# Distance attention of a two-layer decoder: scores by row halves, norms by bf16 pieces

## The chip, the cores and the metric

The kernel runs on one core of a Trainium2 chip. The metric is the time of the device in microseconds (us) for one whole execution. The engines are TensorE (PE, matrix products into the banks of PSUM), VectorE (DVE), ScalarE (ACT) and GpSimd (POOL), each with its own queue of instructions in fixed order; they wait for each other by semaphores. SyncE (SP) issues the DMAs.

## What is computed

A decoder of two layers over x of 4 batches x 512 tokens x 128 features. The change touches only the first attention, which has 16 heads of 64 features and weighs by distance:

```
P = LN(x) @ W_in + b_in                  # per head: Q, K, V, G of 64 features
d2 = q2[:, None] + k2[None, :] - 2 * Q @ K.T
W = (1e-4 + sqrt(max(d2, 0))) ** -2
A = (W / (1e-4 + W.sum(-1))) @ V
x = x + (G * A) @ W_out + b_out
```

q2 and k2 are the squared norms of the rows of Q and K. After it come a cross attention with ReLU, an attention with top-2 experts, and the second layer (window attention, cross attention, a quantized feed-forward); their instructions stay as they are. All matrix products of the first attention are fp32.

## The kernel before

**Units.** Stage A, the distance attention, is cut into 32 units u, one for each pair of heads p of each batch b (`divmod(u, PAIRS)`). A unit has 2 heads x 512 queries x 512 keys. Keys lie on partitions, queries along the free axis, so that a bank (128 keys x 512 queries) is one of eight score chunks c, numbered head by head (`hd, kt = divmod(c, QT)`).

**Scores.** One fp32 product over all 128 rows gives a whole chunk but for k2 (`scores`, L1910). Its 128 contraction rows are, for head 0, the 64 features of K above 64 rows of ones (`SK`), against the 64 features of -2Q above the 64 squares of Q (`MQ`); for head 1 the halves change places. So q2 comes out of the same product. For this the query projection is made twice with the weights written twice into WQ (keys QA and QB, L1891), once for each head with both row halves alike; VectorE scales one half (L2250) and ScalarE squares the other (`squares`, L2078). k2 comes from `key_norms` (L1899), a product of the squared keys with a constant of ones by head halves, and is copied to K2 (L2263).

**From scores to weights.** VectorE adds k2 and takes the maximum with 1e-30 (`guard`, L2272, one instruction a chunk, eight a unit) into D, which has two buffers. ScalarE takes for each head, four chunks together, the square root (L2084), the logarithm (L2092) and the exponential of -2 times it (L2100). Between root and logarithm, and between exponential and root, it loads another table. The logarithm and exponential of the row sums (`row_sums`, L2107 and L2111) and the squares of the next unit stand between the two large logarithms.

**Behind the weights.** GpSimd adds the four key chunks of each head by two instructions, 1024 and 512 columns (`sum_weights`, L2408, L2413). TensorE makes the weighted values (`weighted_values`, L1919, column halves: one head writes partitions 0 to 63, the other 64 to 127 of one bank) and, from GpSimd's sums, the row sums (L1925). ScalarE's inverse of them goes into the gates on GpSimd (`scale_gates`, L2420), VectorE multiplies gates and weighted values (`gated`, L2283), and TensorE adds the pair's piece of the output projection (`out_piece`, L1936).

**Order.** Each engine's order is written out by hand. On TensorE a turn of the loop over u is: scores(u); keys and values of u+1 (L1879, L1882); weighted values and row sums of u-1; queries (twice) and gates of u+1 (L1893), key norms of u+1; output piece of u-2; then the extra jobs of `after_batch`, which carry finished batches into the next layer norm and cross attention. PSUM banks are handed out in that order by `psum_jobs` and `place_jobs`: stage A rotates through banks 0 to 6 (pool A), bank 7 gathers the output pieces. `begin` makes TensorE wait until the reader of a bank's former user is done.

**The end of stage A.** Stage C (attention with experts) begins while the last unit is finished; `TAIL` says at which of its steps n a leftover of stage A is issued: weighted values and row sums of unit 31 (L1919, L1925) at n = 9, the gated values of unit 30 at n = 6. In stage C, L738 and L757 are bf16 products of 32 rows, L1016 reductions of them on VectorE, and L1144 to L1155 GpSimd's steps that split an fp32 operand into bf16 pieces.

## Time and profile before

| | |
|---|---|
| median of 3 timed runs | 1331.55 us (1330.48 to 1332.87) |
| the profiled execution | 1330.9 us, span of its trace 1329.1 us |
| TensorE busy in the span | 1209.8 us, 91% |
| VectorE | 959.5 us, 72% |
| ScalarE | 922.6 us, 69% |
| GpSimd | 509.4 us, 38% |
| chain that ended last | TensorE 78%, VectorE 12% |
| costliest groups | L2272, guards: 189.9 us; L1910, scores: 225.7 us; L2408, sums: 151.2 us |
| DMA | busy in the first two of 40 slices, then hardly |

Busy time is the time in which an engine has an instruction running; products on TensorE overlap, so a group's busy time is that of their union. The chain of waits goes back from the last instruction, at each step to what released it. An fp32 product is two instructions in the trace (x16 is eight products), each with its own load of weights (PEld). A form such as 128*64 128x512 is a product over 128 rows to 64 columns of the array, with 512 columns of the moving operand.

### The profile page before, as it was taken

The page shows a single profiled execution, that of the slowest core. Times are in us where ns is not written, and L with a number is a line of the kernel's source. Part 1 is how long each engine was busy: PE and PEld are TensorE (multiplying, and loading weights), DVE is VectorE, ACT ScalarE, POOL GpSimd, SP SyncE. Part 2 cuts the span into 40 slices and gives each one's busy share as a digit, 9 for nine tenths or more (in the row PEclk, how much of TensorE's full clock was granted, in tenths as well). Part 3 has the DMA queues.
Part 4 walks back from the last instruction along what each step waited for, and adds up shares of the span by engine and source line. Part 5 has one row for each costly group of instructions (what it writes and reads, how often), then busy time and mean ns, then how long its engine had stood idle before and what let it go on. Part 6 is the DMA issues. An engine that isn't in the chain of part 4 may idle for free.

```text
span 1329.1 us, 16572 instructions
## 1 busy us (share of the span) xinstructions
PE 1209.8 (91%) x5870; PEld 658.3 (50%) x5870; DVE 959.5 (72%) x1782; ACT 922.6 (69%) x1194; POOL 509.4 (38%) x359
## 2 busy tenths in 40 slices
PE   6999999999999999998888888899999999976765
PEld 3444544445454445542322222577775777743444
DVE  7876777777777778666888898236546787768895
ACT  3999999999999999993667777545554565633321
POOL 2554444545444545485445452023330000034233
PEclk9999999999999999996989999799998999979778
DMA  8200000000000000010000000000001000000000
GB/s 184 65 1 1 0 0 1 0 0 1 1 1 1 0 0 1 1 64 1 17 1 1 0 2 0 1 1 0 1 0 60 1 1 1 1 1 1 1 8 24
DMA packets 27709, 14.97 MB, mean 11 GB/s; under 512 B 16638, under 2 KB 26476, under 8 KB 27500
## 3 DMA queue, kind: packets, MB, share of 16 engines
q1 hardware_dynamic: 27628, 13.92, 3.9%
q8 instruction: 48, 0.79, 0.3%
q14 instruction: 33, 0.27, 0.1%
HBM read 12.86 MB, written 1.05 MB: 10 GB/s over the span
## 4 chain that ended last, share of the span: by engine, by line
PE 78%; DVE 12%; issue 5%; POOL 2%; ACT 2%; DMA 0%; POOLq 0%; SPq 0%; ACTq 0%; DVEq 0%
PE PS L1910 17%; PE PS L1919 9%; DVE ARENA L1016 5%; PE PS L882 4%; PE PS L1891 4%; PE PS L857 4%; PE PS L771 3%; PE PS L1237 3%; PE PS L722 3%; PE PS L1226 2%; PE PS L1221 2%; PE PS L1213 2%; PE PS L738 2%; PE PS L1936 2%; PE PS L1879 2%
## 5 line engine op out<-in xcount | busy, mean ns | idle before, releaser
L2272 DVE TENSOR_SCALAR ARENA<-PS,ARENA 128x512 f32<-128x512 f32 x256 | 189.9, 749 | 54.9 <-PE PS L1910 36.1
L1910 PE MATMUL PS<-ARENA 128*128 128x512 f32 x512 | 225.7, 594 | 2.4 <-issue 2.3
L2408 POOL TENSOR_TENSOR ARENA<-ARENA 128x1024 f32<-128x1024 f32 x64 | 151.2, 2363 | 126.0 <-ACT ARENA L2100 121.4
L1016 DVE TENSOR_REDUCE ARENA<-PS 128x1 f32<-128x512 f32 x256 | 161.0, 682 | 32.4 <-PE PS L738 32.0
L927 ACT ACTIVATE ARENA<-PS 128x1024 f32<-128x1024 f32 x128 | 128.4, 1026 | 50.2 <-PE PS L757 50.1
L1910 PEld LDWEIGHTS PS<-ARENA 128*128 128x128 f32 x512 | 95.0, 190 | 113.3 <-issue 111.1
L2084 ACT ACTIVATE ARENA<-ARENA 128x2048 f32<-128x2048 f32 x64 | 122.1, 1911 | 31.6 <-DVE ARENA L2272 31.2
L2092 ACT ACTIVATE ARENA<-ARENA,consts_sb 128x2048 f32<-128x2048 f32 x64 | 127.8, 1996 | 0.4
L1919 PE MATMUL PS<-ARENA 128*64 128x512 f32 x512 | 118.3, 604 | 0.9 <-DVE ARENA L2272 0.9
L2100 ACT ACTIVATE ARENA<-ARENA 128x2048 f32<-128x2048 f32 x64 | 118.4, 1898 | 0.0
L2250 DVE TENSOR_SCALAR ARENA<-PS,BT 64x512 f32<-64x512 f32 x64 | 48.0, 750 | 77.7 <-PE PS L1891 74.2
L2420 POOL TENSOR_TENSOR ARENA<-ARENA 128x512 f32<-128x512 f32 x32 | 40.7, 1273 | 162.8 <-ACT ARENA L2111 162.7
L1172 POOL TENSOR_TENSOR ARENA<-ARENA 128x512 f32<-128x512 f32 x32 | 40.6, 1269 | 142.1 <-DVE ARENA L1130 141.9
L738 PE MATMUL PS<-ARENA 32*128 32x512 bf16 x256 | 73.3, 409 | 20.6 <-DVE ARENA L1016 15.1
L2413 POOL TENSOR_TENSOR ARENA<-ARENA 128x512 f32<-128x512 f32 x64 | 82.1, 1283 | 5.0
L771 PE MATMUL PS<-ARENA 128*32 128x512 f32 x512 | 73.6, 648 | 10.6 <-issue 10.4
L963 ACT ACTIVATE ARENA<-PS,BN 128x512 f32<-128x512 f32 x64 | 43.0, 687 | 47.9 <-PE PS L857 47.8
L738 PEld LDWEIGHTS PS<-ARENA 32*128 32x128 bf16 x256 | 18.1, 92 | 102.2 <-DVE ARENA L1016 65.7
L882 PEld LDWEIGHTS PS<-W,ARENA 128*128 128x128 f32 x512 | 61.6, 192 | 12.9 <-issue 12.4
L1617 POOL TENSOR_TENSOR X<-X,W 128x512 f32<-128x512 f32 x4 | 6.0, 1498 | 159.7 <-DVE Y L2214 159.7
L1919 PEld LDWEIGHTS PS<-ARENA 128*64 128x64 f32 x512 | 34.5, 138 | 61.2 <-issue 57.6
L1891 PE MATMUL PS<-XT,WQ 128*128 128x512 f32 x128 | 63.4, 618 | 0.0
(268 smaller groups left out, 2469.7 us busy)
## 6 DMA issues: line engine op xcount, KB each, us to landing
ARENA<-in_window_bias_dram SPq DMA_DIRECT2D x1, 1536.0 KB, 6.6
WKVG<-in_L_attn_W_in_dram SPq DMA_DIRECT2D x3, 448.0 KB, 6.8
X<-in_x_dram SPq DMA_DIRECT2D x4, 256.0 KB, 4.8
W<-in_L_ffn_w_dram SPq DMA_DIRECT2D x1, 1024.0 KB
out_dram<-X SPq DMA_DIRECT2D x4, 256.0 KB, 2.2
WQ<-in_L_attn_W_in_dram SPq DMA_DIRECT2D x2, 448.0 KB, 8.0
BV<-in_L_attn_b_in_dram SPq DMA_DIRECT2D x1, 512.0 KB, 6.8
Wout<-in_L_attn_W_out_dram SPq DMA_DIRECT2D x1, 512.0 KB, 4.8
```

The source lines that it names most:

```text
L738: done(pe.matmul(begin(("cS", n, j)), STK[r, w % 4, 0, t * P:(t + 1) * P], STK[r, w % 4, 1, :], start=True, stop=True), ("cS", n, j))
L882: mm = pe.matmul(o[:, t * P:(t + 1) * P], H1[:, i % 2, c, t * P:(t + 1) * P], W2[:, e, c, :], start=c == 0, stop=c == 1)
L927: act.activation(PT[m % PT_SLOTS], bank(("cP", m)), ACT.Exp, scale=0.5).then_inc(sem("c_exp"), 1)
L1016: dve.tensor_reduce(NMX[:, w % 2, t, h:h + 1], bank(("cS", n, j)), AX.X, ALU.max, negate=True).then_inc(sem("c_max"), 1)
L1891: done(pe.matmul(o, w, XT[:, b], start=True, stop=True), (key, u))
L1910: done(pe.matmul(o, SK[:, hd, kt * P:(kt + 1) * P], MQ[:, hd, :], start=True, stop=True), ("S", u, c))
L1919: mm = pe.matmul(o[hd * 64:hd * 64 + 64, :], VA[:, u % 3, kt, hd * 64:hd * 64 + 64], D[:, u % 2, hd, kt, :], start=kt == 0, stop=kt == QT - 1)
L2084: act.activation(d, d, ACT.Sqrt).then_inc(sem("rooted"), 1)
L2092: act.activation(d, d, ACT.Ln, bias=const("eps_w")).then_inc(sem("logged"), 1)
L2100: act.activation(d, d, ACT.Exp, scale=-2.0).then_inc(sem("w_ready"), 1)
L2272: dve.tensor_scalar(D[:, u % 2, hd, kt, :], bank(("S", u, c)), K2[:, u % 2, kt, hd:hd + 1], 1e-30, ALU.add, ALU.max).then_inc(sem("guarded ...
L2408: pool.tensor_tensor(WPAIR, D[:, u % 2, hd, 0:2], D[:, u % 2, hd, 2:4], ALU.add).then_inc(sem("w_paired"), 1)
```

## The change

- Scores. A chunk is now the sum of two products in one bank: first three bf16 pieces of q2 (32 rows, of which `PIECES` has ones in three; each of four chunks has its own group of 32 rows), then the fp32 product over the 64 rows of a head, head 0 in rows 0 to 63 and head 1 in rows 64 to 127. Chunks are numbered by key block and then head, so heads alternate. Scores come in two groups of four, in each first the four pieces, then the four fp32 products. D has the key block ahead of the head, and ScalarE's two instructions of each kind cover two key blocks of both heads.
- Query norms. Queries are projected once (`project_pair`, with the keys), two units ahead; VectorE makes their square (times -2) from the bank, TensorE sums it by a product with `pairsum` (`query_norms`), VectorE scales it into QX, and GpSimd splits QX into the pieces by four instructions (`split_norms`), three units ahead in its queue. ScalarE's squares are gone; KSQ and QSQ come from `scalar_tensor_tensor` on a bank and SBUF.
- Order. Keys and queries of u+2, values and gates of u+1, weighted values and row sums of u-1, the extra jobs, the norms of u+2, the output piece of u-2. Gated values are those of u-2, ahead of the pair's evacuation. On ScalarE the row sums stand behind both large logarithms, with the extra jobs (`between`) between them and the exponentials. On GpSimd three sums of 1024 columns take the place of two of 1024 and two of 512, and the gates come last in a turn.
- Banks. Pool A has six banks, the weighted values bank 6 alone.
- Start and tail: unit 0 makes the pairs and norms of units 0, 1 and 2; gated30 stands at n = 5 and sums31 at n = 6. One of two DMAs for WQ goes, in each of the two parts of the weights. Scratch tiles share places (MSK with R1, MB with BXV).

The diff, cut; what it takes away is the code printed above.

```diff
+    piece = part % 32
+    cols["piece_drops_high"] = (piece >= 1).astype(np.float32)[:, None]
+    cols["piece_drops_mid"] = (piece == 2).astype(np.float32)[:, None]
+    cols["is_piece"] = (piece < 3).astype(np.float32)[:, None]
...
-TAIL = {"scores2": 1, "values0": 2, "gated30": 6, "sums31": 9, "logits2": 12, "gated31": 13, "out2": 14, "add2": 15,
+TAIL = {"scores2": 1, "values0": 2, "gated30": 5,  "sums31": 6, "logits2": 12, "gated31": 13, "out2": 14, "add2": 15,
...
+    def project_pair(u):
+        return [(("K", u), 1, [("k_sb", u + 1), ("ksq", u + 1)], "A"), (("Q", u), 1, [("mq_scaled", u + 1), ("qsq", u + 1)], "A")]
+
+    def project_values_and_gates(u):
+        return [(("V", u), 1, [("v_sb", u + 1)], "A"), (("G", u), 1, [("g_sb", u + 1)], "A")]
+
+    def query_norms(u):
+        return [(("q2", u), 1, [("q2_sb", u + 1)], "A")]
 
...
+    def scores(u, half):
+        return [(("S", u, c), 1, [("guarded", 8 * u + c + 1)], "A") for c in range(4 * half, 4 * half + 4)]
+
+    jobs += project_pair(0) + project_values_and_gates(0) + query_norms(0) + key_norms(0)
     for u in range(UNITS):
...
+        jobs += scores(u, 0)
+        jobs += scores(u, 1)
+        if u == 0:
+            jobs += project_pair(1) + query_norms(1) + key_norms(1)
+        if u + 2 < UNITS:
+            jobs += project_pair(u + 2)
         if u + 1 < UNITS:
...
+            jobs += project_values_and_gates(u + 1)
         if u >= 1:
...
+            jobs += weighted_values_job(u - 1, "PV" if u + 1 < UNITS else "cV4")
+            jobs += row_sums_job(u - 1, "A" if u + 1 < UNITS else "cP")
...
-POOLS = {"all": range(BANKS), "D": range(0, 6), "DO": range(6, 8), "A": range(0, 7), "out0": range(7, 8), "cS": range(0, 3), "cV4": range(3, 4), "cP": range(4, 8)}
+POOLS = {"all": range(BANKS), "D": range(0, 6), "DO": range(6, 8), "A": range(0, 6), "PV": range(6, 7), "out0": range(7, 8), "cS": range(0, 3), "cV4": range(3, 4), "cP": range(4, 8)}
...
+            def project_pair(u):
                 b, p = divmod(u, PAIRS)
                 o = begin(("K", u))
                 done(pe.matmul(o, wpair(p, 0), XT[:, b], start=True, stop=True), ("K", u))
+                o = begin(("Q", u))
+                w = WQ[:, 0, 2 * p:2 * p + 2, :].rearrange("p h e -> p (h e)")
+                done(pe.matmul(o, w, XT[:, b], start=True, stop=True), ("Q", u))
...
+            def query_norms(u):
+
+                pe.wait_ge(sem("qsq"), u + 1)
+                o = begin(("q2", u))
+                done(pe.matmul(o, const("pairsum"), QSQ, start=True, stop=True), ("q2", u))
...
+            def scores(u, half):
+
+                if half == 0:
+                    pe.wait_ge(sem("q_stack"), u + 1)
+                    pe.wait_ge(sem("mq_scaled"), u + 1)
+                    pe.wait_ge(sem("k_sb"), u + 1)
+                banks = {}
+                for c in range(4 * half, 4 * half + 4):
+                    g = slice(32 * (2 * (c % 2) + c // 2 % 2), 32 * (2 * (c % 2) + c // 2 % 2) + 32)
+                    banks[c] = begin(("S", u, c))
+                    pe.matmul(banks[c], PIECES[g, :], STKQ[g, u % 2, :], start=True, stop=False)
+                for c in range(4 * half, 4 * half + 4):
+                    kt, hd = divmod(c, 2)
+                    r = slice(64 * hd, 64 * hd + 64)
+                    done(pe.matmul(banks[c], SK[r, u % 2, kt * P:(kt + 1) * P], MQ[r, u % 2, :], start=False, stop=True),
                          ("S", u, c))
 
             def weighted_values(u):
...
                 pe.wait_ge(sem("v_sb"), u + 1)
                 o = begin(("PV", u))
                 for kt in range(QT):
+                    if kt % 2 == 0:
+                        pe.wait_ge(sem("w_ready"), 2 * u + kt // 2 + 1)
                     for hd in range(2):
                         mm = pe.matmul(o[hd * 64:hd * 64 + 64, :], VA[:, u % 3, kt, hd * 64:hd * 64 + 64],
...
+                                       D[:, u % 2, kt, hd, :], start=kt == 0, stop=kt == QT - 1)
                 done(mm, ("PV", u))
...
+            def row_sums(u):
+                pe.wait_ge(sem("w_summed"), u + 1)
                 o = begin(("RS", u))
                 for hd in range(2):
...
+            project_pair(0)
+            project_values_and_gates(0)
+            query_norms(0)
             key_norms(0)
+            pe.wait_ge(sem("pieces_set"), 1)
             for u in range(UNITS):
...
+                scores(u, 0)
+                scores(u, 1)
                 if u == 0:
...
+                    pe.wait_ge(sem("win_in"), 16 * 4)
+                    project_pair(1)
+                    query_norms(1)
+                    key_norms(1)
+                if u + 2 < UNITS:
+                    project_pair(u + 2)
                 if u + 1 < UNITS:
...
+                    project_values_and_gates(u + 1)
                 if u >= 1:
                     weighted_values(u - 1)
...
+                    row_sums(u - 1)
...
             def weights(u):
 
                 act.preload_act_table_set("natural_log_exp_and_others")
...
+                for half in range(2):
+                    act.wait_ge(sem("rooted"), 2 * u + half + 1)
+                    act.activation(chunk(u, half), chunk(u, half), ACT.Ln, bias=const("eps_w")).then_inc(sem("logged"), 1)
+                if u >= 1:
+                    row_sums(u - 1)
+                between(u)
+                for half in range(2):
+                    act.wait_ge(sem("logged"), 2 * u + half + 1)
+                    act.activation(chunk(u, half), chunk(u, half), ACT.Exp, scale=-2.0).then_inc(sem("w_ready"), 1)
...
+            def evacuate_pair(u):
 
                 p = u % PAIRS
                 full(dve, ("K", u))
...
+                dve.tensor_scalar(SK[:, u % 2, :], bank(("K", u)), BKP[:, p:p + 1], None, ALU.add
+                                  ).then_inc(sem("k_sb"), 1)
+                full(dve, ("Q", u))
+                dve.tensor_scalar(MQ[:, u % 2, :], bank(("Q", u)), BQP[:, p:p + 1], -2.0, ALU.add, ALU.mult
+                                  ).then_inc(sem("mq_scaled"), 1)
+                dve.wait_ge(sem("k_sb"), u + 1)
+                dve.scalar_tensor_tensor(out=KSQ, in0=bank(("K", u)), scalar=BKP[:, p:p + 1], in1=SK[:, u % 2, :],
+                                         op0=ALU.add, op1=ALU.mult).then_inc(sem("ksq"), 1)
+                dve.wait_ge(sem("mq_scaled"), u + 1)
+                dve.scalar_tensor_tensor(out=QSQ, in0=bank(("Q", u)), scalar=BQP[:, p:p + 1], in1=MQ[:, u % 2, :],
+                                         op0=ALU.add, op1=ALU.mult).then_inc(sem("qsq"), 1)
...
+            def query_norms(u):
+                full(dve, ("q2", u))
+                if u:
+                    dve.wait_ge(sem("q_rest"), u)
+                dve.tensor_scalar(QX, bank(("q2", u)), -0.5, None, ALU.mult).then_inc(sem("q2_sb"), 1)
...
+                kt, hd = divmod(c, 2)
                 if c == 0:
                     dve.wait_ge(sem("k2_sb"), u + 1)
+                    if u >= 2:
+                        full(dve, ("PV", u - 2))
+                        dve.wait_ge(sem("w_paired"), 2 * (u - 2) + 2)
                 full(dve, ("S", u, c))
...
+                dve.tensor_scalar(D[:, u % 2, kt, hd, :], bank(("S", u, c)), K2[:, u % 2, kt, hd:hd + 1], 1e-30,
...
+            full(dve, ("ln", 0, B - 1))
+            evacuate_pair(0)
             dve.wait_ge(sem("bv_in"), 16)
...
+            evacuate_values(0)
             evacuate_gates(0)
+            query_norms(0)
             key_norms(0)
             for u in range(UNITS):
                 for c in range(4):
...
                     guard(u, c)
                 for c in range(4, 8):
                     guard(u, c)
+                if u >= 2:
+                    gated(u - 2)
+                if u == 0:
+                    evacuate_pair(1)
+                    query_norms(1)
+                    key_norms(1)
+                if u + 2 < UNITS:
+                    evacuate_pair(u + 2)
                 if u + 1 < UNITS:
...
+                    evacuate_values(u + 1)
                     evacuate_gates(u + 1)
...
+                if u + 2 < UNITS:
+                    query_norms(u + 2)
+                    key_norms(u + 2)
...
+                pool.wait_ge(sem("w_ready"), 2 * u + 1)
+                if u >= 2:
+                    full(pool, ("RS", u - 2))
+                pool.tensor_tensor(WSUM[:, u % 2], D[:, u % 2, 0], D[:, u % 2, 1], ALU.add).then_inc(sem("w_paired"), 1)
+                pool.wait_ge(sem("w_ready"), 2 * u + 2)
+                if u:
+                    pool.wait_ge(sem("w_summed"), u)
+                pool.tensor_tensor(WPAIR, D[:, u % 2, 2], D[:, u % 2, 3], ALU.add).then_inc(sem("w_paired"), 1)
+                pool.wait_ge(sem("w_paired"), 2 * u + 2)
+                pool.tensor_tensor(WSUM[:, u % 2], WSUM[:, u % 2], WPAIR, ALU.add).then_inc(sem("w_summed"), 1)
+
+            def split_norms(u):
+
+                pool.wait_ge(sem("q2_sb"), u + 1)
+                if u:
+                    pool.wait_ge(sem("q_rest"), u)
+                pool.tensor_scalar(HIQ, QX, const("piece_drops_high"), 0.0, ALU.mult, ALU.add).then_inc(sem("q_high"), 1)
+                pool.wait_ge(sem("q_high"), u + 1)
+                if u:
+                    pool.wait_ge(sem("q_stack"), u)
+                pool.tensor_tensor(R1Q, QX, HIQ, ALU.subtract).then_inc(sem("q_rest"), 1)
+                pool.wait_ge(sem("q_rest"), u + 1)
+                pool.tensor_scalar(MIDQ, R1Q, const("piece_drops_mid"), 0.0, ALU.mult, ALU.add).then_inc(sem("q_mid"), 1)
+                pool.wait_ge(sem("q_mid"), u + 1)
+                if u >= 2:
+                    full(pool, ("S", u - 2, 7))
+                pool.tensor_tensor(STKQ[:, u % 2], R1Q, MIDQ, ALU.subtract).then_inc(sem("q_stack"), 1)
...
+            split_norms(0)
...
+            for u in range(1, 3):
+                split_norms(u)
             for u in range(UNITS):
...
                 sum_weights(u)
+                if u + 3 < UNITS:
+                    split_norms(u + 3)
                 if u in (29, 30):
                     stack(pool, u - 29)
...
+                scale_gates(u)
```

## Rows read from the trace of the kernel before

**Rows 1.** The page's first line.
```profile
span 1329.1 us, 16572 instructions
```

**Rows 2.** Windows view, 300 to 400: busy us by engine, TensorE clock, DMA.
```profile
core 0: us, PE busy (x) PEld busy (x) DVE busy (x) ACT busy (x) POOL busy (x), PEclk, DMA share, GB/s
300.00:400.00 100.00, 100.00 (x388) 50.01 (x387) 73.99 (x124) 93.45 (x74) 47.55 (x28) 1.00 0.00 1
```

**Rows 3.** Chain of waits, one plain unit: start us, length us, engine, line.
```profile
286.20 6.87 PE PS L1910 x16
293.07 0.86 PE PS L1879 x2
293.93 0.89 PE PS L1882 x8
294.82 3.58 PE PS L1919 x16
298.40 0.86 PE PS L1925 x4
299.26 1.91 PE PS L1891 x4
301.18 0.86 PE PS L1893 x2
...
303.82 6.87 PE PS L1910 x16
```

**Rows 4.** Timeline of ScalarE, units 1 and 31: start us, length us.
```profile
43.01 1.28 ACT L2084 ACT_TABLE_LOAD   x1
...
52.59 1.39 ACT L2078 ACTIVATE ARENA<-PS,BT 64x512 f32<-64x512 f32 x2
53.89 1.99 ACT L2092 ACTIVATE ARENA<-ARENA,consts_sb 128x2048 f32<-128x2048 f32 x1
...
59.49 1.28 ACT L2084 ACT_TABLE_LOAD   x1
...
596.61 3.69 ACT L2100 ACTIVATE ARENA<-ARENA 128x2048 f32<-128x2048 f32 x2
```

**Rows 5.** Timeline of TensorE in stage C: start us, length us.
```profile
742.36 0.39 PE L738 MATMUL PS<-ARENA 32*128 32x512 bf16 x1
742.36 0.39 PE L757 MATMUL PS<-ARENA 32*128 32x512 bf16 x2
742.37 0.38 PE L738 MATMUL PS<-ARENA 32*128 32x512 bf16 x1
```

**Rows 6.** Groups by form, TensorE, scores: busy us, mean ns, idle before.
```profile
L1910 PE MATMUL PS<-ARENA 128*128 128x512 f32 x512 | 225.7, 594 | 2.4 <-issue 2.3
...
L1910 PEld LDWEIGHTS PS<-ARENA 128*128 128x128 f32 x512 | 95.0, 190 | 113.3 <-issue 111.1 <-DVE ARENA L2272 1.2 <-DVE ARENA L2250 0.3
```

**Rows 7.** Groups by form, VectorE: guards and gated values.
```profile
L2272 DVE TENSOR_SCALAR ARENA<-PS,ARENA 128x512 f32<-128x512 f32 x256 | 189.9, 749 | 54.9 <-PE PS L1910 36.1
...
L2283 DVE TENSOR_TENSOR ARENA<-PS,ARENA 128x512 f32<-128x512 f32 x32 | 22.1, 691 | 5.7 <-POOL ARENA L2420 2.1
```

**Rows 8.** Groups by form, GpSimd: attention sums, gates, stage C's norm steps.
```profile
L2408 POOL TENSOR_TENSOR ARENA<-ARENA 128x1024 f32<-128x1024 f32 x64 | 151.2, 2363 | 126.0 <-ACT ARENA L2100 121.4
...
L2420 POOL TENSOR_TENSOR ARENA<-ARENA 128x512 f32<-128x512 f32 x32 | 40.7, 1273 | 162.8 <-ACT ARENA L2111 162.7
...
L1147 POOL TENSOR_TENSOR ARENA<-ARENA 128x1024 f32<-128x1024 f32 x16 | 34.1, 2133 | 1.3
...
L1150 POOL TENSOR_SCALAR ARENA<-ARENA,consts_sb 128x512 bf16<-128x512 f32 x32 | 22.5, 715 | 1.6
```

**Rows 9.** Timeline of TensorE: scores of units 0, 2, 31, weighted values 31.
```profile
22.89 7.13 PE L1910 MATMUL PS<-ARENA 128*128 128x512 f32 x16
...
54.39 7.03 PE L1910 MATMUL PS<-ARENA 128*128 128x512 f32 x16
...
580.50 7.03 PE L1910 MATMUL PS<-ARENA 128*128 128x512 f32 x16
...
610.37 5.04 PE L1919 MATMUL PS<-ARENA 128*64 128x512 f32 x16
```

More of the change, by code:

```diff
@@ L1789, in _ @@
                                  .partition_broadcast(P)).then_inc(sem("bv_in"), 16)
-                for half in range(2):
-                    sp.dma_start(WQ[:, heads, half, :], w_in[:, 0, heads]).then_inc(sem(name), 16)
+                sp.dma_start(WQ[:, 0, heads], w_in[:, 0, heads]).then_inc(sem(name), 16)
                 for kind in range(3):
@@ L2323, in _ @@
                 for c in range(4):
-                    if c == 0 and u >= 2:
-                        full(dve, ("RS", u - 2))
                     guard(u, c)
```

241 lines of the change are left out of this document (82 added, 159 removed).

## The prediction

> **What bounds the kernel now.** I read the profiled execution, 1330.9 us, of which the trace holds a span of 1329.1 [rows 1]; the rest, 1.8 us, I carry over unchanged. The median of the three timed runs is 1331.55, 0.65 more. First the busy time by stretches: from 300 to 400 us TensorE is busy 100.00 us of 100 at a granted clock of 1.00 (its level of 2.4 GHz), ScalarE 93.45, VectorE 73.99, GpSimd 47.55 [rows 2]. Then the chain of waits: within a unit (one pair of heads of one batch, 32 in all) it never leaves TensorE [rows 3]. A unit without an extra job runs from 286.20 to 303.82, 17.62 us: scores 6.87, keys 0.86, values 0.89, weighted values 3.58, row sums 0.86, both query projections 1.91, gates 0.86, and key norms and output piece, of the values' shape, 0.89 each. So a microsecond taken from TensorE's unit is worth one, until another engine or another chain is as long. ScalarE is near: from table load to table load, 43.01 to 59.49, it takes 16.48 us without an outside wait [rows 4].
>
> **TensorE.** *Scores.* The eight fp32 products over all 128 rows cost 6.87, 0.86 each. They become products of 64 rows, heads alternating between the upper and lower half of the array. Do halves run side by side? The weighted values do so with column halves: eight products in 3.58, which is 0.90 a pair, of which about 0.1 is the switch of shape, for the full-array products around them take 0.86 [rows 3]. Row groups do so in bf16: four 32-row products start within 0.01 us of each other and all end 0.39 later [rows 5]. No row has fp32 row halves. Bounds: 3.44 us for the four pairs (4 x 0.86) if they overlap like the column halves, 6.87 if not at all. I take 3.44, as both neighbours overlap.
>
> *Norm pieces.* Eight bf16 products of 32 rows, in two groups of four row groups each. Full overlap costs about 0.22 a group (0.39 less 0.17 of emptying the array, under which the next product runs: one of the two passes of an fp32 product lasts 0.594 [rows 6], and they follow each other every 0.43); no overlap costs eight such, 1.8. With four starts at one time in [rows 5] I take 0.22 twice. Each of four switches of shape costs 0.1 (above). Scores then sum to 3.44 + 0.44 + 0.4 = 4.28.
>
> *Banks.* Both groups ask for all four of their banks before the first product. Of six banks, the eighth piece needs the bank of the second score of the same unit. That score ends 0.32 + 0.86 + 0.17 = 1.35 after the unit's first piece; two guards of 0.749 [rows 7] with their starts end at about 2.95, where TensorE stands ready at 2.14. So 0.8 of waiting: the scores cost 5.1. The fourth bank of a unit is that of the row sums before, which ScalarE frees only after its second logarithm; it comes below.
>
> *The others.* Two query projections (1.91) become one (0.86); the query norm is a new full product, 0.86 plus a switch, 0.96. New unit: 17.62 - 6.87 - 1.91 + 5.1 + 0.86 + 0.96 = 15.76.
>
> **The Trainium skill on row groups.** The rows show four bf16 row groups in the time of one [rows 5]. The Trainium skill, TensorE: Matmul & The Clock Gate, section "Measured speedup vs the span model", gives 3.07 for four row tiles, 77% of the ideal. By that share two halves would give 1.54: an estimate from that page of 4.46 for the scores, not 3.44, and 1.0 more a unit. The trace has nothing for fp32, so it stays beside rival C.
>
> **ScalarE.** The two squares go: with their place in the queue they take 53.89 - 52.59 = 1.30. Its pure period becomes 16.48 - 1.30 = 15.18 [rows 4]. Logarithm and exponential of the row sums move behind both large logarithms, at no change in length. The extra jobs move ahead of the exponentials; each is one instruction of 0.6 to 0.7, covered by the 0.6 a unit that ScalarE has over. Without that cover they would cost some 12 such, 8 us in all.
>
> **GpSimd.** Per unit it had two sums of 1024 columns at 2.363, two of 512 and the gates, each like the 1.273 of the gates: 8.6 us. Now three of 1024, 7.09; the gates, 1.27; and four norm steps of 512 columns, two scaled copies at 0.715 and two subtractions at half of 2.13 up to 1.27, so 3.6 to 4.0 [rows 8]. Together about 12.3, and with eight gaps of some 0.06 between them 12.8 of 15.8. Its load isn't the bound, its place in a chain may be: row sums(u-1) on TensorE, then the query norm behind them in the same queue, VectorE's copy, the norm steps, gates(u-1), the sums of unit u, row sums(u). In series: 0.86 + 1.03 + 0.05 + 0.75 + 0.05 + 3.8 + 0.3 + 1.27 + 7.09 + 0.3 = 15.5. It ends at the same point as TensorE's own sequence and is 0.3 shorter; at the high ends (2.38, 1.27, 0.77) it is 15.9.
>
> **VectorE.** Ten instructions beside the guards become nine: two biased keys, two squares of 64 rows, two queries go; one key, one query, two products with a PSUM operand (like the gated values, 0.691 [rows 7]) and the scaled norm come. About 17 x 0.75 = 12.8 of 15.8, no bound. Its chain: first score at 1.35 of the scores' time, eight guards to 7.4, gated values to 8.1, which frees the single bank of the weighted values. TensorE gets there at 5.1 + 0.86 + 0.86 + 0.89 + 0.86 = 8.6. It fits by 0.5.
>
> **The fourth bank.** In times after TensorE's start of row sums(u-1): they are in the bank at 1.0, the next scores start at 3.6. The eighth guard ends at about 11.1, ScalarE's second root at 13.0, table and both logarithms at 18.1, which is 2.4 of the next unit (period 15.7); the row-sum logarithm ends at 3.1, before 3.6. It fits by 0.5. The weights are ready at 3.1 + 0.65 + 3.8 = 7.6, before GpSimd wants them at 8.1 and TensorE at 12.2.
>
> So four chains lie at 15.2, 15.5, 15.8 and, the last two, within 0.5 of it. Bounds of the plain unit: 15.2 (ScalarE alone) and 18.3 (no overlap). I take 15.9, TensorE's 15.76 and 0.15 for collisions.
>
> **Start and end.** Before, scores 0, 2 and 31 start at 22.89, 54.39 and 580.50 [rows 9]. From 54.39 to 580.50 are 29 units: 526.1 = 29 x 17.62 + 15.1; these 15.1 are the extra jobs on TensorE's queue, which stay. At the start the first scores now wait for the squares of the query, its norm, the copy and the four steps on GpSimd: about 3.8 later, 26.7. Norms of units 1 and 2 are then made one after the other, behind GpSimd's biases and memsets, with nothing to hide them, and the first sums stand behind the norms of unit 2. By the same durations scores 2 start at about 58, 3.6 later; bounds 0 (TensorE already stands before scores 1 now, which may hide it) and 7. Scores 31 then start at 58 + 29 x 15.9 + 15.1 = 534.2, 46.3 earlier.
>
> At the end weighted values 31 start on TensorE at 610.37 though their weights were there at 600.3 [rows 4, 9]; three steps earlier in the queue (n = 6 for 9) they start 0 to 6 earlier. Their row sums still need GpSimd's two pair sums and two more, so I take 3. The rest of the kernel keeps its instructions. Sum: 1329.1 - 46.3 - 3 + 1.8 = 1281.6, so 1282.
>
> **Rivals.**
> A, the forecast: 1282, by itself 1268 to 1298.
> B, GpSimd's chain sets the unit: a copy on VectorE that comes late, or its steps slowed by VectorE beside it (the 1024-column sum is 2.363 in this stage and 2.13 in the other [rows 8]), adds 0.8: 16.7, + 23 us, 1305. For it: the chain is only 0.3 shorter. Against: all its steps have rows.
> C, halves overlap only in part. An fp32 product loads weights twice, 0.190 each [rows 6]. If two loads a pair stand bare, a pair costs 1.24 for 0.86: 1.5 a unit, 44 us, 1326; the page's share above would give 1.0 a unit, 1311. Against: the values' products, eight such loads, take 0.89 in all [rows 3].
> D, no overlap, and slower: fp32 products of row halves run one after the other. The change then doesn't do what it says. Scores cost 6.87 + 0.44 + 0.4, the unit 17.62 - 8.78 + 7.71 + 1.82 = 18.37; 29 x 0.75 = 22, with start and end 1330.9 + 21.8 + 3.6 - 3 = 1353. It decides from scores of 7.0 us a unit upward.
> E, better: the bank wait of 0.8 is covered, TensorE's unit is 15.0, and ScalarE's 15.2 sets it: 29 x 0.7 = 20 less, 1262.
>
> **How the numbers follow.** A 0.54, B 0.15, C 0.10, D 0.12, E 0.09. A measurement of this kernel can tell about 0.2%, 2.7 us, from no change. Faster: A, B, E and half of C, 0.83. C reaches up to the time before: 0.04 for the same, 0.01 for slower; with D 0.13. The range 1257 to 1323 holds A, B, E and most of C; D is outside.
>
> **What would show it.** The chain of the new kernel between 280 and 340 should have scores of about 5.1, one query projection, and a unit of 15.9; the timeline of TensorE two scores of different heads starting together, one short wait for a guard between the halves; ScalarE busy 97% and in the chain now and then. First scores near 26.7, third near 58. A wait of TensorE for GpSimd's sum before the row sums means B, scores of 6.5 or more C, of 7.7 D. I am wrong if the unit is under 15.0 or over 16.5, or if a stage behind this one changes by more than 5 us.

## The result and the profile after

The changed kernel takes 1303.14 us (median of 4 runs, 1298.57 to 1303.7), the kernel before on the same chip 1332.21. The ratio is 0.9781, its 95% interval 0.9764 to 0.9798: 2.2% faster, 29 us. The forecast was 1282: the direction and the main mechanism, the row halves side by side, came out, and 21 of the 50 us did not. The profiled execution took 1303.17.

From the page of the kernel after: its span, the engines' busy time, the chain of waits by engine, and two groups that answer to [rows 6, 8].

```profile
span 1301.3 us, 17124 instructions
PE 1161.3 (89%) x6126; PEld 614.8 (47%) x6126; DVE 914.4 (70%) x1753; ACT 876.4 (67%) x1130; POOL 618.7 (48%) x455
PE 36%; POOL 30%; issue 19%; DVE 13%; ACT 1%; POOLq 0%; DMA 0%; SPq 0%; ACTq 0%; DVEq 0%
L1954 PE MATMUL PS<-ARENA 64*128 64x512 f32 x512 | 130.9, 631 | 0.0
L2466 POOL TENSOR_TENSOR ARENA<-ARENA 128x1024 f32<-128x1024 f32 x32 | 76.0, 2375 | 2.5
```

The 512 passes of the fp32 score products are busy for 130.9 in all, where those over the whole array had 225.7 [rows 6]. The chain of waits now puts 30% of the span down to GpSimd, as rival B would have it; e2 shows below that this is a misreading.

The same stretch of a plain unit as in [rows 3], from TensorE's timeline of the kernel after. The columns are start, length (to the modelled end, so that neighbours overlap by about 0.17), line, forms and count; in brackets the wait before and what ended it. Lines 1950 and 1954 are the norm pieces and the score products, 1911 the key (query, values and gates, 317.15 to 319.85, are left out; the gates alone, from 318.90, take 0.95), 1964 the weighted values, 1972 the row sums, 1930 the query norm, 1936 the key norms, 1983 the output piece.

```profile
310.90 0.40 PE L1950 MATMUL PS<-ARENA,PIECES 32*128 32x512 bf16 x4
311.23 1.99 PE L1954 MATMUL PS<-ARENA 64*128 64x512 f32 x8
313.15 0.53 PE L1950 MATMUL PS<-ARENA,PIECES 32*128 32x512 bf16 x3
313.95 0.39 PE L1950 MATMUL PS<-ARENA,PIECES 32*128 32x512 bf16 x1 [0.27 <-DVE ARENA L2320]
314.27 1.99 PE L1954 MATMUL PS<-ARENA 64*128 64x512 f32 x8
316.19 1.13 PE L1911 MATMUL PS<-XT,WKVG 128*128 128x512 f32 x2
...
319.85 3.65 PE L1964 MATMUL PS<-ARENA 128*64 128x512 f32 x16
323.34 1.03 PE L1972 MATMUL PS<-ARENA,consts_sb 128*64 128x512 f32 x4
324.30 1.12 PE L1930 MATMUL PS<-Y,consts_sb 128*128 128x512 f32 x2
325.26 1.05 PE L1936 MATMUL PS<-consts_sb,ARENA 128*128 128x128 f32 x8
326.15 1.06 PE L1983 MATMUL PS<-Wout,ARENA 128*128 128x128 f32 x8
327.14 0.40 PE L1950 MATMUL PS<-ARENA,PIECES 32*128 32x512 bf16 x4
```

From piece to piece the unit takes 16.24 (310.90 to 327.14), where it took 17.62. Four products in two row halves take 1.92; before, the eight products over the whole array took 6.87 [rows 3]. The scores as a whole take 5.29 (310.90 to 316.19). There is one hole, 0.80 from 313.15 to 313.95: the eighth piece waits for the bank that a guard (line 2320) empties.

Windows of the kernel after: busy time of TensorE, its weight loads, VectorE, ScalarE and GpSimd, then the granted clock. The second line answers to [rows 2].

```profile
200.00:300.00 100.00, 98.36 (x467) 45.07 (x466) 68.22 (x109) 93.26 (x65) 72.83 (x49) 1.00 0.00 1
300.00:400.00 100.00, 96.81 (x460) 44.41 (x458) 70.59 (x126) 89.02 (x64) 68.88 (x47) 0.98 0.00 1
```

### The profile page after: what moved, and what is told of

Its sections match the earlier page's. It is cut to its first block, busy times and chain, and to the rows that moved or that the text cites. A ratio compares the mean times of both kernels' runs of the same rounds, so it can differ in the third digit from the quotient of the medians.

```text
span 1301.3 us, 17124 instructions
## 1 busy us (share of the span) xinstructions
PE 1161.3 (89%) x6126; PEld 614.8 (47%) x6126; DVE 914.4 (70%) x1753; ACT 876.4 (67%) x1130; POOL 618.7 (48%) x455
## 4 chain that ended last, share of the span: by engine, by line
PE 36%; POOL 30%; issue 19%; DVE 13%; ACT 1%; POOLq 0%; DMA 0%; SPq 0%; ACTq 0%; DVEq 0%
DVE ARENA L1048 6%; POOL ARENA L2466 6%; POOL ARENA L2464 6%; POOL ARENA L2460 6%; PE PS L914 4%; PE PS L889 4%; POOL WQ L2477 3%; POOL ARENA L2490 3%; PE PS L803 3%; PE PS L1269 3%; PE PS L1258 2%; PE PS L1253 2%; PE PS L1245 2%; PE PS L770 2%; PE PS L754 2%
## 5 line engine op out<-in xcount | busy, mean ns | idle before, releaser
L2320 DVE TENSOR_SCALAR ARENA<-PS,ARENA 128x512 f32<-128x512 f32 x256 | 174.6, 744 | 67.8 <-PE PS L1954 67.3
L2133 ACT ACTIVATE ARENA<-ARENA 128x2048 f32<-128x2048 f32 x64 | 122.2, 1911 | 62.3 <-DVE ARENA L2320 61.8
L1954 PE MATMUL PS<-ARENA 64*128 64x512 f32 x512 | 130.9, 631 | 0.0
L2140 ACT ACTIVATE ARENA<-ARENA,consts_sb 128x2048 f32<-128x2048 f32 x64 | 124.6, 1994 | 0.4
L1204 POOL TENSOR_TENSOR ARENA<-ARENA 128x512 f32<-128x512 f32 x32 | 40.6, 1270 | 142.0 <-DVE ARENA L1162 141.9
L2473 POOL TENSOR_SCALAR WQ<-ARENA,consts_sb 128x512 bf16<-128x512 f32 x32 | 22.3, 695 | 159.8 <-DVE ARENA L2296 159.8
L2296 DVE TENSOR_SCALAR ARENA<-PS 128x512 f32<-128x512 f32 x32 | 22.1, 692 | 95.0 <-PE PS L1930 95.0
L2466 POOL TENSOR_TENSOR ARENA<-ARENA 128x1024 f32<-128x1024 f32 x32 | 76.0, 2375 | 2.5
L2464 POOL TENSOR_TENSOR ARENA<-ARENA 128x1024 f32<-128x1024 f32 x32 | 75.8, 2369 | 0.0
L2460 POOL TENSOR_TENSOR ARENA<-ARENA 128x1024 f32<-128x1024 f32 x32 | 75.7, 2365 | 0.0
L1954 PEld LDWEIGHTS PS<-ARENA 64*128 64x128 f32 x512 | 45.3, 191 | 46.2 <-issue 46.2
```

Of the source, the lines that this page charges most:

```text
L1954: done(pe.matmul(banks[c], SK[r, u % 2, kt * P:(kt + 1) * P], MQ[r, u % 2, :], start=False, stop=True), ("S", u, c))
L2133: act.activation(chunk(u, half), chunk(u, half), ACT.Sqrt).then_inc(sem("rooted"), 1)
L2140: act.activation(chunk(u, half), chunk(u, half), ACT.Ln, bias=const("eps_w")).then_inc(sem("logged"), 1)
L2320: dve.tensor_scalar(D[:, u % 2, kt, hd, :], bank(("S", u, c)), K2[:, u % 2, kt, hd:hd + 1], 1e-30, ALU.add, ALU.max).then_inc(sem("guarded ...
L2460: pool.tensor_tensor(WSUM[:, u % 2], D[:, u % 2, 0], D[:, u % 2, 1], ALU.add).then_inc(sem("w_paired"), 1)
L2464: pool.tensor_tensor(WPAIR, D[:, u % 2, 2], D[:, u % 2, 3], ALU.add).then_inc(sem("w_paired"), 1)
```

## Where the 21 us lie

The execution splits at three marks: the pieces of scores 2, of scores 31, and the end.

| part | forecast | measured | more |
|---|---|---|---|
| up to scores 2 | 58 | 63.53 | 5.5 |
| 29 plain units | 29 x 15.9 | 29 x 16.24 | 9.9 |
| extra jobs of these units | 15.1 | 18.2 | 3.1 |
| behind scores 31 | 3 less than before | 748.61 (before 748.60) | 3.0 |

Together 21.5, and 1281.6 + 21.5 is the 1303.1 measured. The 18.2 is what is left of 489.16, the way from scores 2 to scores 31 at 552.69, once 29 x 16.24 is taken off. The parts are those of one profile. A second profile of the same kernel (e10) has 62.92, 488.28 and 749.2, so they are good to about 1 us. The last part varies more between kernels that are alike there, by 7 us (last section), so its 3.0 is the least certain.

## The experiments

All are edits of the changed kernel. Ratios are to the kernel before, run on the same chip.

**e1: are the two row halves really side by side?** Both heads read the same upper half.

```diff
-                    r = slice(64 * hd, 64 * hd + 64)
+                    r = slice(0, 64)
```

> Left out: head 1's own scores, since the fp32 products of both heads read rows 0 to 63. Everything else is the changed kernel. Theory 1 (the row halves run side by side, which is where the gain of the scores comes from): two products in the same rows follow each other, each group of four costs 3.5 to 3.6 us instead of 1.92, the wait of 0.80 for the guard goes, since VectorE keeps pace; the plain unit grows from 16.24 to about 18.8, the whole by 29 x 2.6 = 75, to 1375 to 1385. Rival (a product over 64 rows is cheaper by itself): the unit stays at 16.2 and the time at 1303.

Measured: 1395.5 (2 runs, 1385.79 and 1405.21), ratio 1.0469 (1.0381 to 1.0558). TensorE's timeline of e1:

```profile
301.40 3.70 PE L1954 MATMUL PS<-ARENA 64*128 64x512 f32 x8
305.03 0.39 PE L1950 MATMUL PS<-ARENA,PIECES 32*128 32x512 bf16 x4
305.36 3.70 PE L1954 MATMUL PS<-ARENA 64*128 64x512 f32 x8
308.98 0.70 PE L1911 MATMUL PS<-XT,WKVG 128*128 128x512 f32 x1
```

A group of four takes 3.63 instead of 1.92, and the bank wait of 0.80 is covered. The unit is 18.86; 2 x 1.71 - 0.80 = 2.62 more, as it should be. The whole is longer than the 1375 to 1385 expected, since two units with an extra job take 29.71 and 30.51: around the first of them, from 400 to 440, the granted clock is 0.79, behind a wait of 1.77. Less 0.2 that each group pays for the switch of shape (e3 measures it), the groups are 3.43 and 1.72: halves overlap fully. Rivals C and D are out, and the row halves are worth more than the whole change: without them it loses.

**e2: is GpSimd's chain the bound?** The third sum of 1024 columns becomes one of 64.

```diff
-    pool.tensor_tensor(WSUM[:, u % 2], WSUM[:, u % 2], WPAIR, ALU.add)
+    pool.tensor_tensor(WSUM[:, u % 2, 0, 0:64], WSUM[:, u % 2, 0, 0:64], WPAIR[:, 0, 0:64], ALU.add)
```

> Left out: all but 64 columns of GpSimd's third sum, so the row sums lack half of the weights. Theory 1 (TensorE's own queue sets the unit; GpSimd is done about 1 us before TensorE takes the row sums): plain unit 16.24 as before, time 1303 within 2, although GpSimd loses 2.3 us of 12.2 a unit. Rival (the chain through GpSimd's norm steps and sums sets it, as the chain of waits of the changed kernel says with 30% on GpSimd): the unit falls to where the next bound is, 15.5 or less, the time to 1280 or less.

Measured: 1305.2 (4 runs, 1303.34 to 1309.05), ratio 0.9796 (0.9772 to 0.9819), the unit 16.24 as before. Windows and the page's chain of e2:

```profile
200.00:300.00 100.00, 98.33 (x466) 45.01 (x465) 68.32 (x109) 93.03 (x65) 59.96 (x49) 1.00 0.00 1
...
PE 72%; DVE 18%; issue 6%; POOL 2%; ACT 1%; DMA 0%; POOLq 0%; DVEq 0%; SPq 0%; ACTq 0%
```

GpSimd has 13 us less in every 100 and nothing moves. The chain's 30% of GpSimd falls to 2% and TensorE's 36% rises to 72% at the same time. So the chain of the changed kernel walked one of two paths of nearly equal length. GpSimd's timeline of the kernel after gives the slack:

```profile
319.94 2.37 POOL L2466 TENSOR_TENSOR ARENA<-ARENA 128x1024 f32<-128x1024 f32 x1
326.25 0.70 POOL L2473 TENSOR_SCALAR WQ<-ARENA,consts_sb 128x512 bf16<-128x512 f32 x1 [3.94 <-DVE ARENA L2296]
```

The last sum ends at 322.31, TensorE wants it at 323.34: 1.03 to spare. Rival B, whose time of 1305 was the nearest of all to the result, is wrong by its mechanism.

**e3: the bank wait and the switches.** The second half of the scores goes in two pairs, pieces and products, so that the eighth piece asks for its bank later.

```diff
-                for c in range(4 * half, 4 * half + 4):
+                for chunks in ([range(0, 4)] if half == 0 else [range(4, 6), range(6, 8)]):
+                    for c in chunks:
...
-                for c in range(4 * half, 4 * half + 4):
+                    for c in chunks:
```

> In the second half of the scores pieces and products come in two pairs (pieces 4 and 5, products 4 and 5, pieces 6 and 7, products 6 and 7). Theory 1 (the 0.80 us in which the eighth piece waits for the second guard is time of the unit): the wait goes, 0.2 for two more switches and 0.2 for a second start of pieces come; unit 15.8 to 15.9, time 1291 to 1295. Rival (VectorE's and GpSimd's chains stand right behind): the wait comes back at another place, unit 16.2, time 1302 to 1304.

Measured: 1293.53 (4 runs, 1290.97 to 1300.31), ratio 0.9712 (0.9679 to 0.9745). TensorE's timeline of e3:

```profile
320.85 0.40 PE L1951 MATMUL PS<-ARENA,PIECES 32*128 32x512 bf16 x4
321.18 1.99 PE L1955 MATMUL PS<-ARENA 64*128 64x512 f32 x8
323.10 0.39 PE L1951 MATMUL PS<-ARENA,PIECES 32*128 32x512 bf16 x2
323.41 1.13 PE L1955 MATMUL PS<-ARENA 64*128 64x512 f32 x4
324.48 0.39 PE L1951 MATMUL PS<-ARENA,PIECES 32*128 32x512 bf16 x2
324.79 1.13 PE L1955 MATMUL PS<-ARENA 64*128 64x512 f32 x4
325.85 1.12 PE L1911 MATMUL PS<-XT,WKVG 128*128 128x512 f32 x2
```

No wait is left; the scores take 5.00 instead of 5.29 and the unit 15.95. A pair of products takes 1.07 (323.41 to 324.48), a group of four 1.92: 0.86 a pair and about 0.2 once for each group, however many products are in it. That measures the switch by itself. The wait of 0.80 went, a second group of pieces and its switches cost 0.5 of it, and 0.29 x 29 = 8.4 is the gain in the plain part of the units, of 9.6 between the medians. The 29 units together fall by 9.7, from 489.16 to 479.45; the other 1.3 lies in units with an extra job, which I have not taken apart.

**e4: the two long units.** Of the 29 units two are 3.5 and 3.3 longer than a plain one (from 361.11 and from 498.50). TensorE's timeline of the kernel after, then VectorE's:

```profile
361.11 0.39 PE L1950 MATMUL PS<-ARENA,PIECES 32*128 32x512 bf16 x3
363.25 0.38 PE L1950 MATMUL PS<-ARENA,PIECES 32*128 32x512 bf16 x1 [1.75 <-DVE X L2346]
```

```profile
360.40 2.19 DVE L2258 TENSOR_SCALAR Y<-X,MV,RSTD 128x128 f32<-128x128 f32 x4
362.52 0.68 DVE L2346 SCALAR_TENSOR_TENSOR X<-PS,X 128x512 f32<-128x512 f32 x1
```

The fourth bank holds the cross-attention output; VectorE adds it to X (line 2346) only behind a normalization of 2.19, and the pieces now ask for four banks at once. In the first of the two the granted clock falls as well, to 0.91 from 360 to 380.

The change lengthened that normalization too. VectorE's timeline of the kernel before, then of e9, the run without the four norm steps on GpSimd:

```profile
412.04 1.11 DVE L2214 TENSOR_SCALAR Y<-X,MV,RSTD 128x128 f32<-128x128 f32 x4
```

```profile
328.12 1.12 DVE L2253 TENSOR_SCALAR Y<-X,MV,RSTD 128x128 f32<-128x128 f32 x4
```

In both GpSimd has nothing running beside it; in the kernel after it runs its norm steps for 2.0 of the 2.19. The five normalizations between 220 and 560 us take 2.19 to 2.22 in the kernel after and 1.10 or 1.11 in the kernel before. So up to about 1.1 of the wait of 1.75 comes from GpSimd's new work, an estimate from these rows (2.19 less 1.11). e4 puts the addition ahead of the norms and the normalization.

```diff
+                if after_batch(u, 10) is not None:
+                    add_cross(after_batch(u, 10), with_stats=False)
                 if u + 2 < UNITS:
                     query_norms(u + 2)
...
-                    add_cross(after_batch(u, 10))
+                    stats(2, after_batch(u, 10))
```

> VectorE adds the cross attention to the stream (which frees the fourth bank of the next scores) ahead of the copies of the norms and of the layer norm's scaling, not behind them. Theory 1 (two units of 31, those from 361.11 and 498.50, lose 1.75 us of waiting each to this bank, one of them 1.7 more to a clock that falls to 1.2 GHz): both become as long as their neighbours with a like job, 17.2 to 17.3; time 4 to 5 less, 1298 to 1299. Rival (the copy of the query norm comes later by the 0.7 us of the addition and hands the loss to GpSimd's chain): at most 1 less.

Measured: 1299.6 (4 runs, 1296.5 to 1302.98), ratio 0.9758 (0.9731 to 0.9785). The units fall from 19.71 to 17.62 and from 19.53 to 18.40, the 29 together from 489.16 to 486.28. In this pair of profiles that is 2.9 of the 3.1 that the extra jobs cost beyond the forecast. Against the second profile of the changed kernel (e10), where the first of the two units takes 18.78, it is 2.0. Between the medians, whose runs lie 5 apart, it is only just to be seen.

**e5 and e11: the tail's order as it was.** The values' product of the last unit goes back to its old place.

```diff
-"gated30": 5,  "sums31": 6
+"gated30": 6, "sums31": 9
```

> Weighted values and row sums of unit 31 back to step 9 of stage C, gated values of unit 30 back to step 6. In the changed kernel the last scores are followed by 748.61 us, before by 748.60, although these weighted values start 22.3 us after the scores and not 29.9. Theory 1 (what the earlier place gained was lost again by a collision: four small instructions of VectorE, the split of the first maxima, took 6.9 us in all under GpSimd's gates, memsets and norm steps, where before they took 1.0 beside idle time of GpSimd): with the old place they take 1 us again, and the rest stays at 748 to 750; time within 2 of 1303. Rival (the earlier place gained nothing and the 6.9 us have another cause): they stay long, and the rest grows to 752 or more.

> Weighted values and row sums of unit 31 at step 9, gated values of unit 30 at step 6, once more, with five rounds beside the changed kernel. Theory 1 (the earlier place costs time, since stage C's first maxima wait under GpSimd's work): 2 to 4 us faster than the changed kernel. Rival (stage C makes good what its start loses or gains, and the 3 us between the first measurements are the spread of the runs): the same within 1.5 us.

e5 gave 1300.1 (4 runs, 1299.09 to 1303.59), ratio 0.9749 (0.9723 to 0.9775), 3 less than the first median of the change. That looked like a loss by the new place, so it was run again beside the changed kernel itself (e10):

> The changed kernel unaltered, timed beside the next two on one chip. Both theories: 1303 by the runs so far, with single runs between 1298 and 1304, which is the spread against which a tail of 3 us has to be seen.

e10, the change once more: 1302.43 (5 runs, 1298.12 to 1304.43). e11: 1301.96 (4 runs, 1299.4 to 1304.06). Half a microsecond apart, so the medians show no loss by the new place, and the 3 us of e5 can be the spread of the runs. The profiles show more than the medians. With the old place the four small instructions take 2.2 in all in e5, not 6.8, and the first windows of stage C are ahead: the 73rd of its 256 reductions (line 1048) starts 90.8 us behind scores 31 in e5 and 90.9 in e11, but 95.9 in the changed kernel. By the last of the 256 that lead is gone (250.3 and 250.5, against 249.8). So the new place does cost its first windows 5 us, and stage C makes up for it. Both kernels with the old place still end earlier, 745.1 and 745.2 behind scores 31 where the changed kernel has 748.6 and 749.2, but e4, with the new place, has 744.5, so this can't be put down to the place. But the gain of 3 that I forecast isn't there either: in the changed kernel weighted values 31 do start 22.26 behind scores 31 (574.95 against 552.69), where it was 29.87 [rows 9], and the kernel ends 748.61 behind scores 31, where it was 748.60. They were not what the end of the stage waits for. What the runs can't tell is a gain or loss of a microsecond or two.

**e6: a memset in the way of the next stage.** From VectorE's timeline of the kernel after, then GpSimd's:

```profile
582.91 3.31 DVE L1055 CAST ARENA<-ARENA 128x16 bf16<-128x16 f32 x1
...
587.61 2.20 DVE L1058 TENSOR_TENSOR ARENA<-ARENA 128x16 bf16<-128x16 f32 x1
```

```profile
583.90 2.27 POOL L2512 MEMSET ARENA<- 128x2048 f32 x2
...
587.60 2.12 POOL L1179 TENSOR_TENSOR ARENA<-ARENA 128x1024 f32<-128x1024 f32 x1
```

Four VectorE instructions of 128x16 (two of them shown) take 3.31, 0.62, 0.66 and 2.20, 6.8 together, where the kernel before has 0.25, 0.18, 0.20 and 0.23 for the same four, and the first and the last of them end as an instruction of GpSimd does (at 586.2 and near 589.8). e6 moves the memsets behind the third stack:

```diff
-            for t in (VC1, AOT):
-                pool.memset(t, 0.0).then_inc(sem("c_init"), 1)
             pool_c(pool)
... in the loop of the stacks
+                if w == 2:
+                    for t in (VC1, AOT):
+                        pool.memset(t, 0.0).then_inc(sem("c_init"), 1)
```

> GpSimd's two memsets at the end of stage A stand behind the norm steps of window 2, not ahead of them. Theory 1 (VectorE's small instructions each wait until GpSimd's current instruction is over, and window 2's pieces come 2.3 us late): the first of the four is done 2 to 3 us sooner and the pieces of window 2 too, the time behind the last scores falls by 2 to 3, to 1300 or 1301. Rival (that stretch is bound elsewhere): no difference.

Measured: 1303.59 (4 runs, 1301.87 to 1304.79), ratio 0.9768 (0.9748 to 0.9787): no change. The four are back at 1.11, 0.18, 0.20 and 0.23, so the cause is right (the 1.11 ends with GpSimd's gates), and the 5.1 us are worth nothing in the end. They aren't lost at once: the last of stage C's 256 reductions starts 246.0 behind scores 31, 3.8 earlier than in the changed kernel, and only in the stages after it is the lead used up; the kernel ends 748.6 behind scores 31, as before. What bounds those stages I have not looked into.

**e7: the start.** Projections and norms of unit 1 go ahead of scores 0 on TensorE and VectorE, and its pieces ahead of the biases on GpSimd.

```diff
             key_norms(0)
+            pe.wait_ge(sem("win_in"), 16 * 4)
+            project_pair(1)
+            query_norms(1)
+            key_norms(1)
... on VectorE the same, on GpSimd
             split_norms(0)
+            split_norms(1)
```

> The pair, query norm and key norm of unit 1 are made before the scores of unit 0 on TensorE and VectorE, and GpSimd splits the norm of unit 1 ahead of its biases. Theory 1 (my start was 5.5 us too short because the norms of units 1 and 2 stand one behind the other in the open, with the clock down to 1.2 GHz for the idle time): they fill the 4 us in which TensorE waits for the first pieces; scores 1 start at 40 to 42 and not at 48.22, time 1295 to 1297. Rival (the weights of the other heads arrive only after 27 us): scores 0 start that much later, and at most 3 us are won.

Measured: 1300.37 (4 runs, 1297.88 to 1303.09), ratio 0.9745 (0.972 to 0.977). Scores 0, 1 and 2 start at 29.09, 41.56 and 56.87, where they started at 26.93, 48.22 and 63.53. Of these 6.7 only 2.8 are seen between the medians, 5.4 between the profiled spans and 5.2 at scores 31. Part of it is lost at once, in TensorE's timeline of e7:

```profile
56.87 0.39 PE L1949 MATMUL PS<-ARENA,PIECES 32*128 32x512 bf16 x3
58.54 0.39 PE L1949 MATMUL PS<-ARENA,PIECES 32*128 32x512 bf16 x1 [1.27 <-ACT ARENA L2151]
```

TensorE comes to the fourth bank before ScalarE has taken the logarithm of the row sums out of it.

**e8 and e12: the edits together.** e8 is e3, e4, e6 and e7; e12 has the old tail order instead of the later memsets.

> The pairs of the run with scores in pairs, the early addition of the cross attention, the early start and the late memsets together. Theory 1 (all are parts of one queue, TensorE's, and add up): 1303 - 10 - 4 - 7 - 2 = 1280, plain unit 15.95. Rival (some of the parts hide the same wait): 1287 or more.

> Scores in pairs, early addition of the cross attention, early start, and the tail as in the kernel before. Theory 1 (the tail's place matters): 1280 to 1281. Rival (it doesn't): 1283 to 1284, as the run with the late memsets.

e8: 1283.21 (4 runs, 1282.64 to 1284.7), ratio 0.9618 (0.96 to 0.9636). e12: 1283.5 (4 runs, 1281.33 to 1284.99), ratio 0.9648 (0.9629 to 0.9668), beside 1302.43 for the change itself: 19 us or 1.5% faster than the change, 47 us or 3.5% faster than the kernel before. In the profiles scores 31 start 11.3, 2.8 and 5.2 earlier in e3, e4 and e7 than in the changed kernel, 19.2 in all, and 19.2 earlier in e8 (533.54 for 552.69): the gains add up. Behind scores 31, e8 and e12 take 747.4 and 747.9 for 748.6, so neither the tail's order nor the memsets add more than a microsecond; no run has the three edits alone.

**e9: what the bf16 norms cost.** Pieces, query norm, copy and GpSimd's four steps are left out.

```diff
-                    pe.matmul(banks[c], PIECES[g, :], STKQ[g, u % 2, :], start=True, stop=False)
...
-                o = begin(("q2", u))
-                done(pe.matmul(o, const("pairsum"), QSQ, start=True, stop=True), ("q2", u))
```

> Left out: the query norm's whole path, that is the eight bf16 pieces, the product that sums the squares, VectorE's copy and GpSimd's four steps (the scores lack q2). Theory 1 (TensorE's queue sets the unit, and ScalarE is the next bound, 15.18 by its instructions before): TensorE's unit would be 16.24 - 0.96 - 0.65 = 14.6, ScalarE stops it at 15.2 to 15.4; the start is 4 us shorter; time 1265 to 1273. Rival (ScalarE's waits for the guards, 0.5 and 1.0 us a unit in the changed kernel, are part of its unit): 15.7 or more, time 1280 or more.

Measured: 1255.57 (2 runs, 1251.56 and 1259.58), ratio 0.944 (0.9402 to 0.9477); I had forecast 1265 to 1273. ScalarE's timeline of e9:

```profile
287.16 1.28 ACT L2128 ACT_TABLE_LOAD   x1
...
302.24 1.28 ACT L2128 ACT_TABLE_LOAD   x1
```

From table load to table load 15.08, with 0.09 of it idle: here ScalarE is the bound, and my 15.18 for it was right. It is busy for 99.40 of the 100 us from 200. TensorE's units without an extra job are 14.8 and those with one 15.5 and more, so that it falls back in one and catches up in the next; within the scores it waits 0.8 and more for a guard. The time lies below the 1265 to 1273 because both gains were larger than I had put them: in the profile scores 2 come 10.3 earlier than in the changed kernel (53.24), not 4, and the 29 units take 450.31, 38.9 less and not some 30. Of these 450.31, 29 x 15.08 are 437.3, so the extra jobs add 13.0 here and not 18.2. Behind scores 31 the kernel takes 5.4 more, 754.0, which I have not explained. The norm path costs 47 us of the change (1302.43 less 1255.57). This is what rival E was about: below 15.1 a unit only ScalarE's work is left to cut.

## Why the prediction came out so

*Row halves and row groups: right.* Four pieces start together and cost 0.33; halves overlap fully (e1). Here it is worth weighing the rule that the prediction left beside the sum. The groups of four took 1.72 without the switch and 3.43 when serial (e1), a factor of 2.0; with the switch it is 3.63 to 1.92, 1.89. The Trainium skill, TensorE: Matmul & The Clock Gate, section "Measured speedup vs the span model", has 77% of the ideal for four row tiles; that share does not carry over to two fp32 halves here.

*The bank wait: right,* 0.8 forecast, 0.80 measured. Its parts were off against each other: the guards' pitch is 0.66, not 0.75, but the first one starts 1.59 behind the unit's first piece, not 1.35. TensorE too was ready later, at 2.25 and not 2.14. That the errors cancel is luck.

*The switch of shape: the step that failed.* The term "each of four switches of shape costs 0.1" was mis-sized. The timeline shows 0.1 to 0.3 for a change of shape. Against the bare durations (0.22 for a group of pieces is the forecast's own estimate), each of the two groups of pieces takes 0.1 more (0.33 for 0.22), each of the two groups of products 0.2 (1.92 for 1.72), and each of four others, from start to start, 0.1: the output piece (0.99), the key (0.96), the row sums (0.96), the query norm (0.96). That is 1.0 a unit; the way into the weighted values, 0.1 at the gates, comes on top, but the kernel before pays it too. Seven changes in a unit thus cost 1.1, about 0.16 each. The 0.2 of a group of products isn't owed to the pieces: in e9, which has none, the second group of four still takes 1.92 (285.34 to 287.26). I had counted 0.5: four tenths in the scores and one at the query norm. 15.76 + 0.5 is the 16.24 within rounding. I had put 0.15 for collisions and there were none, so 0.34 a unit is missing, 9.9 in all. The row that tells it stood in [rows 3]: the two query projections took 1.91, 0.19 over 2 x 0.86, and I took the plain end of that row instead of asking where the 0.19 came from. The Trainium skill, TensorEngine Tiling (Array Packing), section "Key Properties", says that a change of tiling mode drains TensorE. The trace agrees, and has the price: 0.1 to 0.3 for a change, 0.16 on average.

*The start: mis-sized.* Scores 0 came at 26.93 (forecast 26.7). From there the norms of units 1 and 2 lie open, which I had priced at full clock and partly hidden. The windows of the kernel after:

```profile
20.00:30.00 10.00, 5.67 (x22) 2.77 (x22) 3.15 (x7) 0.00 (x0) 6.86 (x7) 0.78 0.55 130
30.00:40.00 10.00, 7.32 (x22) 2.27 (x19) 7.97 (x12) 5.83 (x4) 5.32 (x5) 0.84 0.74 212
40.00:50.00 10.00, 9.59 (x45) 5.86 (x43) 5.98 (x11) 8.05 (x5) 5.42 (x6) 0.87 0.01 2
```

and TensorE's timeline:

```profile
26.93 0.74 PE L1950 MATMUL PS<-ARENA,PIECES 32*128 32x512 bf16 x4 [4.00 <-issue]
27.60 3.79 PE L1954 MATMUL PS<-ARENA 64*128 64x512 f32 x8
...
38.71 1.56 PE L1930 MATMUL PS<-Y,consts_sb 128*128 128x512 f32 x2 [2.68 <-DVE Y L2282]
40.06 1.91 PE L1936 MATMUL PS<-consts_sb,ARENA 128*128 128x128 f32 x8
```

TensorE stands for 4.00 and 2.68, and behind each stop it works at half its clock, 1.2 GHz, for a while: the first group of products takes 3.72 for 1.92, and behind the second stop the query norm takes 1.35 for 0.96, the key norms 1.71 for 0.89 and the key 1.31 for 0.96, 1.6 in all. The granted clock of the windows is 0.78 to 0.87. How the rest of the 5.5 divides between slow work and the stops isn't settled, since work late ahead of a stop shortens the stop. In e7, with another order and the same work, scores 2 start at 56.87: it is the order that costs.

*Extra jobs: a step that was missing.* I had them stay at 15.1. Two of them hold the bank that the grouped pieces ask for (e4), 2.0 to 2.9 of the 3.1. A part of it is the normalization in front of that bank: I had asked whether VectorE would slow GpSimd's norm steps (rival B), and it was VectorE's normalization beside them that doubled, from 1.11 to 2.19.

*The end: wrong.* The term "so I take 3" had no reason behind it: the weights' being there early was no evidence that the end of the stage waits for weighted values 31. They started 7.6 earlier and the end stayed where it was; putting them back changed the median by 0.5 (e10, e11).

*The chains that lay close: right.* ScalarE's 15.2 was 15.08 (e9), GpSimd's 15.5 was 15.2 (16.24 less the 1.03 of slack), and the fourth bank, free 1.26 ahead of the next scores in a plain unit (325.88 for 327.14, forecast 0.5), is late where a unit comes early (e7).

*The rivals.* The range 1257 to 1323 was said to hold most of C, but C's own price, 1326, lies outside it.

## What to carry to other kernels

Where products change their tile shape in a tight loop, count the changes into and out of each shape and read their price from two neighbours in the trace. A group that asks for all its banks at once can turn a hidden guard into a wait: here a second half in two pairs was better than one group of four, and no smaller groups were tried. Work moved to GpSimd can lengthen VectorE's work beside it, so look at both timelines. Price an order at the start with the clock that a stop leaves behind. When the chain of waits names an engine, look how long before its use that engine's last result was there, before you believe it.

## What the hardware showed that I had not expected

- A change of TensorE's tile shape costs 0.1 to 0.3 us. A group of fp32 products of two halves pays about 0.2 once: it takes 1.92 for two pairs and 1.07 for one, with 0.86 a pair (e3).
- Some VectorE instructions that work from SBUF to SBUF wait for GpSimd's: a cast of 128x16 took 3.31 us beside GpSimd's memsets and 0.25 in the kernel before, four scalings of 128x128 took 2.19 beside its norm steps and 1.11 without. The Trainium skill, SBUF — State Buffer, section "SBUF: two separate sides", has this as a lock on a shared pair of ports, held for a whole instruction; the ends that coincide (e6) agree with it, though the cast stood through the end of the gates and both memsets, three instructions and not one.
- Of kernels that are alike behind scores 31, the ends lie 744.5 (e4) to 751.6 us (e3) behind them. Single runs of the changed kernel lie between 1298.1 and 1304.4. A gain under 3 us isn't told from one median; what makes this spread stays open.
